# Moving two up-projection slices of the next expert ahead of the broadcast matmuls in an eight-expert feed-forward kernel

## The chip, the cores and the metric

The kernel runs on the 8 cores of one Trainium2 chip, two dies of four cores. All cores run the same program on different data and do not talk to each other. The metric is the device time of the slowest core in microseconds. TensorE is called PE in the profile, VectorE DVE, ScalarE ACT, GpSimd POOL and SyncE SP.

## The reference

```python
def reference(...):
    x = L0_attn_x                      # (4, 4096, 1024)
    x = x + _L0_attn_ref(_layernorm(x), Wd, bd, Wi, bi, gamma, beta)   # gated diagonal scan over time
    x = x + _L0_ffn_ref(_layernorm(x), router_w, w1, b1, w2, b2, gamma, beta)
...
# _L0_ffn_ref, 8 experts, every expert computed for every token, D = 1024, D_FF = 4096
    gates = ...                        # softmax over the top 2 of 8 router logits, 0 elsewhere
    h = gelu(einsum('nd,edf->enf', x, w1) + b1)
    out = einsum('enf,efd->end', h, w2) + b2
    res = x[None] + out
    mu, var = mean(res), mean(square(res - mu))
    expert_out = (res - mu) * rsqrt(var + 1e-6) * gamma + beta
    y = einsum('end,ne->nd', expert_out, gates)
```

The change touches only the expert part. For each expert it needs two big products, a normalization of each token over its 1024 features, and a sum over experts weighted by the gates.

## The kernel before

Each core owns 2048 tokens and first runs the scan stage (about the first 800 us). Then come the experts, in two groups of GT = 1024 tokens (`for g in range(n_groups)`), and in each group 8 experts (`for ee in range(n_experts)`). Features lie on the partitions and tokens on the free axis, so the means over the features are made by matmuls with a column of ones.

The kernel is written against a small recorder (`Rec`). `r.emit(engine, ...)` appends an instruction to one engine's list ("t" PE, "v" DVE, "s" ACT), `r.dma("y"/"q", ...)` a transfer issued by SP or POOL, and `r.wait(engine, token)` a semaphore wait. Each engine runs its own list strictly in the order in which it was written down. So the place of a Python statement sets its place in each engine's queue and nothing else.

One pass of the expert loop, expert `ee`:

- **B(ee)**, L885: out = w2 * h. Per half `th` of 512 tokens it takes 16 blocks `kb` of w2, each of 2 x 8 matmuls: 256 matmuls of 128x512 per half, 512 per expert. The 8 PSUM banks hold the 8 feature tiles, bank `m2` for tile `m2`, in the order 0 to 7. The first matmul into each bank waits on `bank_free[m2]`. DVE moves the sums out as `res_b` (L894, 8 per half).
- **A(ee+1), slice 0**: `emit_A_ms(ee + 1, 0)`. A slice of the up-projection is 128 matmuls (L836) in 16 runs of 8, which take banks 4 and 5 in turn; after each run ACT writes a 128x512 piece of `h_b` by Gelu (L842) and frees the bank. An expert has four slices `ms`.
- The gates of the expert are transposed into a row (L911) and copied to `g_r` (L916). Sums over res_b (L928) and over its squares (L936 on ACT, L945 on PE) go to banks 0 to 3, row 0.
- **A(ee+1), slice 1**, behind these on PE.
- **Row chain**, `rows_combine` (helper, lines 226 to 258) and three more: mean and variance of 1024 tokens in one row on DVE (L237 to L240), square root on ACT (L245), reciprocal (L249) and nm_r (L250) on DVE, then u1, u2 and the gate row in bf16 (L960, L962, L964). Their token is `urows_v`.
- **Broadcast**, L971: 6 matmuls with a row of ones spread u1, u2 and g over 128 partitions, into banks 0 to 3, 6 and 7. The first waits on `urows_v`.
- **y pass**, L982, L984, L987, L992 on DVE: 16 times these four operations of 128x512, which read the broadcast banks and add the expert's weighted output to `yacc`. Its last token is `y_v`:

```python
            y_v = r.token("v")
            res_read_tok = y_v
            prev_y_v = y_v
            for b_ in (0, 1, 2, 3, 6, 7):
                bank_free[b_] = y_v
```

- **A(ee+1), slices 2 and 3**, the last in the pass. Then B(ee+1) begins; it needs `h_done_s` and, in its first matmuls, the banks 0 to 7.

The last expert of a group has no A(ee+1), so there are 7 x 2 = 14 passes with one and 2 without. In these two the y pass is followed by the transposes of the output (L1029).

Weights: w1 comes in slices of 1024 columns into two buffers (`prefetch_w1`, issued at the head of the slice before it: POOL in group 0, which converts from f32, L623, and SP stores the bf16 copy to DRAM, L629; SP in group 1, L635). w2 comes in 16 blocks per half into three buffers (`prefetch_w2`: POOL L650 for the first half in group 0, otherwise SP L662).

Of the kernel before, what the change touches and what calls it, by code (L numbers as in the profile page):

```python
# [111 lines left out]
def build_nc(n_tiles=N_SST, n_groups=NG, n_experts=E, taps=None):  # L112
# [25 lines left out]
    r = Rec(nc, stack)  # L138
# [4 lines left out]
    def tap(name, ap, tok):  # L143
        if name not in tap_set:
            return
        dt_ = ap.dtype
        dr = nc.dram_tensor("tap_" + name, list(ap.shape), dt_,
                            kind="ExternalOutput").ap()
        r.wait("y", tok)
        ttok = r.dma("y", "ost", lambda e, dr=dr, ap=ap: e.dma_start(dr, ap))  # L150
        for engk in ("t", "v", "s", "q", "y"):
            r.wait(engk, ttok)
# [31 lines left out]
    def bank(i):  # L184
        return pall[:, i * 512:(i + 1) * 512]
# [430 lines left out]
    def prefetch_w1(ee, ms, g):  # L616
        par = w1_round[0] % 2
        r.wait("q", w1_free[par])
        r.wait("y", w1_free[par])
        r.wait("q", w1_slot_store[par])  # L620
        r.wait("y", w1_slot_store[par])
        if g == 0:
            tok = r.dma("q", f"w1{par}", lambda e, ee=ee, ms=ms, par=par: e.dma_start(  # L623
                w1bufs[par][:].rearrange("p (kk f) -> p kk f", kk=FC),
                w1[ee, :, ms * 1024:(ms + 1) * 1024].rearrange(
                    "(kk p) f -> p kk f", p=128)))
            r.wait("y", tok)
            stok = r.dma("y", f"w1s{par}", lambda e, ee=ee, ms=ms, par=par:
                         e.dma_start(w1s_dram[ee, ms], w1bufs[par][:]))  # L629
            w1s_tok[(ee, ms)] = stok  # L630
            w1_slot_store[par] = stok
        else:
            r.wait("y", w1s_tok[(ee, ms)])
            tok = r.dma("y", f"w1h{par}", lambda e, ee=ee, ms=ms, par=par:
                        e.dma_start(w1bufs[par][:], w1s_dram[ee, ms]))  # L635
        w1_round[0] += 1
        return tok, par
# [39 lines left out]
    for g in range(n_groups):  # L677
# [135 lines left out]
        def emit_A_ms(ee, ms):  # L813
            nonlocal w1tok, w1par
            cur_tok, cur_par = w1tok, w1par
            if ms < 3:
                w1tok, w1par = prefetch_w1(ee, ms + 1, g)
            elif ee < n_experts - 1:
                w1tok, w1par = prefetch_w1(ee + 1, 0, g)
            elif g == 0 and NG > 1:  # L820
                w1tok, w1par = prefetch_w1(0, 0, 1)
            else:
                w1tok, w1par = None, None
            r.wait("t", cur_tok)
            r.wait("t", xn2_v)
            for m in range(FC):
                for nt in range(2):
                    b_ = 4 + (m * 2 + nt) % 2
                    r.wait("t", bank_free[b_])
                    for kk in range(FC):  # L830
                        lhs = w1bufs[cur_par][:, kk * 1024 + m * 128:
                                              kk * 1024 + (m + 1) * 128]
                        rhs = xn2_b[:, kk * GT + nt * 512:
                                    kk * GT + nt * 512 + 512]
                        r.emit("t", lambda e, l=lhs, rr=rhs, b_=b_, kk=kk:
                               e.matmul(bank(b_), l, rr, start=(kk == 0),  # L836
                                        stop=(kk == FC - 1)))
                    mm_t = r.token("t")
                    fo = ms * 8 + m
                    r.wait("s", mm_t)  # L840
                    r.emit("s", lambda e, fo=fo, nt=nt, b_=b_, ee=ee:
                           e.activation(  # L842
                               h_b[:, fo * 1024 + nt * 512:
                                   fo * 1024 + nt * 512 + 512],
                               bank(b_), AF.Gelu,
                               bias=b1_c[:, ee * 32 + fo:ee * 32 + fo + 1]))
                    bank_free[b_] = r.token("s")
            w1_free[cur_par] = r.token("s")
# [4 lines left out]
        h_done_s = r.token("s")  # L853
        a_mm_tok = r.token("t")

        for ee in range(n_experts):
# [44 lines left out]
            last_in_group = ee == n_experts - 1  # L901
# [62 lines left out]
            r.emit("v", lambda e: e.tensor_copy(g_rb[0:1, :], g_r[0:1, :]))  # L964
            urows_v = r.token("v")

            r.wait("t", urows_v)
            for nt in range(2):
                for b0, row in ((0, u1_rb), (2, u2_rb), (6, g_rb)):
# [28 lines left out]
            prev_y_v = y_v  # L998
            for b_ in (0, 1, 2, 3, 6, 7):
                bank_free[b_] = y_v  # L1000

            if not last_in_group:
                for ms in range(2, 4):
                    emit_A_ms(ee + 1, ms)
                h_done_s = r.token("s")
                a_mm_tok = r.token("t")
            tap(f"res_b{g}_{ee}", res_b[:], res_v)
            tap(f"g_r{g}_{ee}", g_r[0:1, :], urows_v)
            tap(f"rs_r{g}_{ee}", rs_r[0:1, :], urows_v)
# [93 lines left out]
```

How the kernel before makes its waits and increments, by code:

```python
            def body(e):  # L93
                done = 0
                for kind, fn, name, val in self.ops[eng_key]:
                    if kind == "wait":
                        e.wait_ge(self.sems[name], val)
                    else:
                        if ser and kind == "op" and done > 0:
                            e.wait_ge(own, done)
                        fn(e).then_inc(self.sems[name], val)
                        if kind == "op":
                            done += val
```

## Time and profile before

| | |
|---|---|
| median of 2 runs | 5792.02 us (5790.36 to 5793.69) |
| profiled execution, own time | 5787.88 us |
| its span, first to last instruction, slowest core (core 4) | 5786.0 us |
| spans of the 8 cores | 5766.1 to 5786.0 us |
| PE busy | 4373.2 us, 76% of the span |
| DVE, ACT busy | 1663.6 and 1125.9 us |

The page gives one execution on the slowest core. A group row names line, engine, operation and tiles; then busy time and mean of one, and the idle time of the engine just before them with what ended it. Matmuls are pipelined: the listed length of one (about 380 ns) is longer than its step from one to the next. The timeline merges neighbours, so a row may stand for many instructions.

### The profile page before, as it was taken

To read this page: it belongs to the slowest core of one execution; us is meant where nothing else is said; L and a number is where in the kernel's file an instruction comes from. 1 tells how busy PE (TensorE), PEld (TensorE's weight loads), DVE (VectorE), ACT (ScalarE), POOL (GpSimd) and SP (SyncE) were. 2 spreads that over 40 slices of the span, in tenths; PEclk is the share of its full clock that TensorE was granted. 3 is DMA by queue.
4 is the path that set the end of the run, shared out by engine and by line. 5 is a ranking of instruction groups with operands and counts; after the bars stand their busy time and mean duration, and the time that the engine had idled before them with its cause. 6 is when DMAs were issued, how large, how long until landed. Compare 5 with 4: busy or idle time off the path is not lost.

```text
span 5786.0 us, 49875 instructions; the slowest of 8 cores (5766.1 to 5786.0 us)
## 1 busy us (share of the span) xinstructions
PE 4373.2 (76%) x18678; PEld 1883.7 (33%) x19040; DVE 1663.6 (29%) x2165; ACT 1125.9 (19%) x1429; POOL 161.7 (3%) x199
## 2 busy tenths in 40 slices
PE   1874516888888888888787527989888888889893
PEld 0321202333333333333333213434333333334341
DVE  0456532022221313131313351040413140413225
ACT  0332312020212121212111003031212122121210
POOL 0001000000000000000000000000000000000000
PEclk9997758989898989999999758999999999989896
DMA  6100042847475656574746211313132222223231
GB/s 75 44 30 15 29 102 59 185 113 171 120 162 129 157 131 153 127 164 115 166 123 138 77 73 51 124 62 127 65 110 80 95 95 87 94 89 102 80 95 40
DMA packets 229019, 586.59 MB, mean 101 GB/s; under 512 B 75056, under 2 KB 75184, under 8 KB 220592
## 3 DMA queue, kind: packets, MB, share of 16 engines
q1 hardware_dynamic: 157568, 444.95, 22.1%
q0 software_dynamic: 71216, 138.44, 15.6%
q8 instruction: 156, 2.56, 0.2%
q14 instruction: 79, 0.65, 0.0%
HBM read 570.77 MB, written 150.99 MB: 125 GB/s over the span
## 4 chain that ended last, share of the span: by engine, by line
PE 67%; DVE 14%; DMA 9%; ACT 4%; issue 3%; SPq 2%; DVEq 0%; ACTq 0%; POOLq 0%
PE pall L836 31%; PE pall L885 26%; DMA w2buf<-w 7%; PE pall L424 3%; DVE res_b L894 3%; DVE rs_r L249 3%; ACT sq_b L936 2%; PE pall L945 2%; DMA yacc<-xmid_scr 1%; PE pall L928 1%; SPq L201 1%; PE pall L334 1%; DVE xn_b L387 1%; PE pall L971 1%; DVE nm_r L250 1%
## 5 line engine op out<-in xcount | busy, mean ns | idle before, releaser
L885 PE MATMUL pall<-h_b,w2buf 128*128 128x512 bf16 x8020 | 1858.9, 389 | 230.9 <-DMA w2buf<-w 136.5
L836 PE MATMUL pall<-xn_b,w1buf 128*128 128x512 bf16 x8026 | 1849.1, 392 | 144.7 <-ACT h_b L842 67.0
L842 ACT ACTIVATE h_b<-pall,b_c 128x512 bf16<-128x512 f32 x1024 | 703.3, 688 | 3026.0 <-PE pall L836 3025.6
L885 PEld LDWEIGHTS pall<-h_b,w2buf 128*128 128x128 bf16 x8192 | 807.1, 100 | 1282.7 <-issue 392.7
L836 PEld LDWEIGHTS pall<-xn_b,w1buf 128*128 128x128 bf16 x8192 | 818.1, 100 | 1185.6 <-issue 283.3
L894 DVE SCALAR_TENSOR_TENSOR res_b<-pall,b_c,xn_b 128x512 bf16<-128x512 f32 x256 | 192.2, 751 | 2296.0 <-PE pall L885 2271.6
L424 PE MATMUL pall<-xn_b,WdWi_b 128*128 128x512 bf16 x1000 | 236.1, 395 | 128.8 <-ACT dec L434 70.4
L249 DVE RECIPROCAL rs_r<-rs_r 1x1024 f32<-1x1024 f32 (+1 forms) x30 | 157.8, 5261 | 503.6 <-ACT rs_r L245 503.6
L971 PE MATMUL pall<-u_rb,ones_row_b 1*128 1x512 bf16 x64 | 33.0, 616 | 244.8 <-DVE g_rb L964 244.8
L987 DVE SCALAR_TENSOR_TENSOR yacc<-sq_b,fgam_c,yacc 128x512 f32<-128x512 f32 x256 | 192.3, 751 | 29.6 <-DVE sq_b L984 3.7
L992 DVE SCALAR_TENSOR_TENSOR yacc<-pall,fbet_c,yacc 128x512 f32<-128x512 f32 x256 | 192.2, 751 | 26.7
L982 DVE TENSOR_TENSOR sq_b<-res_b,pall 128x512 f32<-128x512 bf16 x256 | 176.1, 688 | 73.6 <-PE pall L971 48.6
L936 ACT ACTIVATE sq_b<-res_b 128x2048 bf16<-128x2048 bf16 x64 | 122.1, 1908 | 381.1 <-DVE res_b L894 276.8
L424 PEld LDWEIGHTS pall<-xn_b,WdWi_b 128*128 128x128 bf16 x1024 | 101.6, 101 | 264.2 <-issue 157.1
L984 DVE TENSOR_TENSOR sq_b<-sq_b,pall 128x512 f32<-128x512 f32 x256 | 176.0, 688 | 26.7
L945 PE MATMUL pall<-sq_b,ones_col_b 128*1 128x512 bf16 x256 | 92.7, 501 | 103.8 <-ACT sq_b L936 103.8
L916 DVE COPY g_r<-pall 1x1024 f32<-1x1024 f32 x16 | 19.4, 1212 | 407.5 <-PE pall L911 407.5
L314 PE MATMUL pall<-ident,xt 128*128 128x128 f32 x256 | 40.7, 307 | 118.7 <-DMA xt<-ssm_x 110.1
L237 DVE COPY nm_r<-pall 1x1024 f32<-1x1024 f32 (+1 forms) x30 | 29.9, 998 | 344.1 <-PE pall L945 232.7
L650 POOL DMA_DIRECT2D w2buf<-w x128 | 90.1, 705 | 1178.1 <-PE pall L885 1122.4
L1029 PE MATMUL pall<-ident,yacc 128*128 128x128 f32 x128 | 28.1, 406 | 125.2 <-DVE yacc L992 106.2
L460 DVE TENSOR_TENSOR_SCAN states<-dec,carry,inj 128x512 f32<-128x512 f32 x64 | 82.1, 1284 | 81.8 <-ACT inj L439 78.3
(104 smaller groups left out, 1235.8 us busy)
## 6 DMA issues: line engine op xcount, KB each, us to landing
w2buf<-w2s_scr SPq DMA_DIRECT2D x384, 512.0 KB, 3.7
w1buf<-w POOLq DMA_DIRECT2D x32, 2048.0 KB, 16.0
w1s_scr<-w1buf SPq DMA_DIRECT2D x32, 2048.0 KB, 6.3
w2buf<-w POOLq DMA_DIRECT2D x128, 512.0 KB, 8.3
w2s_scr<-w2buf SPq DMA_DIRECT2D x128, 512.0 KB, 6.6
w1buf<-w1s_scr SPq DMA_DIRECT2D x32, 2048.0 KB, 7.9
xt<-ssm_x SPq DMA_DIRECT2D x8, 2048.0 KB, 9.3
xmid_scr<-x_f SPq DMA_DIRECT2D x4, 2048.0 KB, 7.2
```

The source lines that it names most:

```text
L249: r.emit("v", lambda e: e.reciprocal(rs_r[0:1, 0:n], rs_r[0:1, 0:n]))
L424: r.emit("t", lambda e, l=lhs, rr=rhs, b_=b_, kk=kk: e.matmul(bank(b_), l, rr, start=(kk == 0), stop=(kk == FC - 1)))
L836: e.matmul(bank(b_), l, rr, start=(kk == 0), stop=(kk == FC - 1)))
L842: e.activation(h_b[:, fo * 1024 + nt * 512: fo * 1024 + nt * 512 + 512], bank(b_), AF.Gelu, bias=b1_c[:, ee * 32 + fo:ee * 32 + fo + 1]))
L885: e.matmul(bank(m2), l, rr, start=(kk2 == 0), stop=(kk2 == 31)))
L894: e.scalar_tensor_tensor(res_b[:, sl], bank(m2), b2_c[:, ee * 8 + m2:ee * 8 + m2 + 1], xn2_b[:, sl], ALU.add, ALU.add))
L936: r.emit("s", lambda e, half=half: e.activation(sq_b[:], res_b[:, half * 2 * GT:(half + 1) * 2 * GT], AF.Square))
L945: r.emit("t", lambda e, rr=rhs, fcg=fcg, nt=nt: e.matmul(pall[0:1, 1024 + nt * 512: 1024 + nt * 512 + 512], ones_col_b[:], rr, start=(fcg ...
L982: r.emit("v", lambda e, sl=sl, nt=nt: e.tensor_tensor(tscr[:, 0:512], res_b[:, sl], bank(0 + nt), ALU.mult))
L984: r.emit("v", lambda e, nt=nt: e.tensor_tensor(tscr[:, 0:512], tscr[:, 0:512], bank(2 + nt), ALU.add))
L987: e.scalar_tensor_tensor(yacc[:, sl], tscr[:, 0:512], fgam_c[:, ee * 8 + fc:ee * 8 + fc + 1], yacc[:, sl], ALU.mult, ALU.add))
L992: e.scalar_tensor_tensor(yacc[:, sl], bank(6 + nt), fbet_c[:, ee * 8 + fc:ee * 8 + fc + 1], yacc[:, sl], ALU.mult, ALU.add))
```

## The change

The block that emits slices 2 and 3 of the next expert's up-projection is moved from behind the y pass to a place ahead of the wait on `urows_v`. Nothing is added or removed. Lines 967 to 1000 of the file shift by six in the new version (the broadcast is L977 there, the y pass L988 to L998).

```diff
@@ -964,6 +964,12 @@
             r.emit("v", lambda e: e.tensor_copy(g_rb[0:1, :], g_r[0:1, :]))
             urows_v = r.token("v")
 
+            if not last_in_group:
+                for ms in range(2, 4):
+                    emit_A_ms(ee + 1, ms)
+                h_done_s = r.token("s")
+                a_mm_tok = r.token("t")
+
             r.wait("t", urows_v)
             for nt in range(2):
                 for b0, row in ((0, u1_rb), (2, u2_rb), (6, g_rb)):
@@ -998,12 +1004,6 @@
             prev_y_v = y_v
             for b_ in (0, 1, 2, 3, 6, 7):
                 bank_free[b_] = y_v
-
-            if not last_in_group:
-                for ms in range(2, 4):
-                    emit_A_ms(ee + 1, ms)
-                h_done_s = r.token("s")
-                a_mm_tok = r.token("t")
             tap(f"res_b{g}_{ee}", res_b[:], res_v)
```

The queue of PE over one pass before, from B of one expert to B of the next (u_rb stands for u1_rb and u2_rb, xn_b for xn2_b, a row for as many equal matmuls as its x says):

```order
L885 MATMUL pall<-h_b,w2buf 128x512 x512
L836 MATMUL pall<-xn_b,w1buf 128x512 x128
L911 MATMUL pall<-ident,gates_tok 1x128 x8
L928 MATMUL pall<-res_b,ones_col_b 1x512 x16
L945 MATMUL pall<-sq_b,ones_col_b 1x512 x16
L836 MATMUL pall<-xn_b,w1buf 128x512 x128
L971 MATMUL pall<-u_rb,ones_row_b 128x512 x2
L971 MATMUL pall<-g_rb,ones_row_b 128x512
L971 MATMUL pall<-u_rb,ones_row_b 128x512 x2
L971 MATMUL pall<-g_rb,ones_row_b 128x512
L836 MATMUL pall<-xn_b,w1buf 128x512 x256
L885 MATMUL pall<-h_b,w2buf 128x512 x512
```

The same stretch of PE's queue in the changed kernel:

```order
L885 MATMUL pall<-h_b,w2buf 128x512 x512
L836 MATMUL pall<-xn_b,w1buf 128x512 x128
L911 MATMUL pall<-ident,gates_tok 1x128 x8
L928 MATMUL pall<-res_b,ones_col_b 1x512 x16
L945 MATMUL pall<-sq_b,ones_col_b 1x512 x16
L836 MATMUL pall<-xn_b,w1buf 128x512 x384
L977 MATMUL pall<-u_rb,ones_row_b 128x512 x2
L977 MATMUL pall<-g_rb,ones_row_b 128x512
L977 MATMUL pall<-u_rb,ones_row_b 128x512 x2
L977 MATMUL pall<-g_rb,ones_row_b 128x512
L885 MATMUL pall<-h_b,w2buf 128x512 x512
```

The 256 matmuls of slices 2 and 3 have moved from behind the six broadcasts to ahead of them, and the broadcasts now stand directly before B.

The second place is the seam before B, with the waits that each instruction carries (`__v` is DVE's semaphore, `__s` ACT's, w22 that of a w2 buffer), as a piece of the difference:

```order
 L836 MATMUL pall<-xn_b,w1buf 128x512 [waits __s]
 L836 MATMUL pall<-xn_b,w1buf 128x512 x7
+L977 MATMUL pall<-u_rb,ones_row_b 128x512 [waits __v]
+L977 MATMUL pall<-u_rb,ones_row_b 128x512
+L977 MATMUL pall<-g_rb,ones_row_b 128x512
+L977 MATMUL pall<-u_rb,ones_row_b 128x512 x2
+L977 MATMUL pall<-g_rb,ones_row_b 128x512
 L885 MATMUL pall<-h_b,w2buf 128x512 [waits w22,__s,__v]
 L885 MATMUL pall<-h_b,w2buf 128x512 x15
```

B's first matmul carries a wait on DVE in both kernels; what moved is that the broadcasts, on which DVE's y pass waits, now come immediately ahead of it. The queues of ACT, POOL and SP are the same in both, and DVE's differs in line numbers only.

## Rows read from the trace of the kernel before

**Rows 1.** The page: busy time by engine, and the chain that ended last, by line.

```profile
PE 4373.2 (76%) x18678; PEld 1883.7 (33%) x19040; DVE 1663.6 (29%) x2165; ACT 1125.9 (19%) x1429; POOL 161.7 (3%) x199
PE pall L836 31%; PE pall L885 26%; DMA w2buf<-w 7%; PE pall L424 3%; DVE res_b L894 3%; DVE rs_r L249 3%; ACT sq_b L936 2%; PE pall L945 2%; DMA yacc<-xmid_scr 1%; PE pall L928 1%; SPq L201 1%; PE pall L334 1%; DVE xn_b L387 1%; PE pall L971 1%; DVE nm_r L250 1%
```

**Rows 2.** Who waited for whom, whole span: us in total, times, longest.

```profile
PE pall L971 <- DVE g_rb L964: 244.8, 16, 18.1
...
PE pall L885 <- DMA w2buf<-w: 136.5, 83, 3.9
...
PE pall L1029 <- DVE yacc L992: 106.2, 2, 53.3
...
PE pall L836 <- ACT h_b L842: 67.0, 16, 31.0
```

**Rows 3.** Timeline, a pass of group 1: slice 1, row chain, broadcast, slice 2.

```profile
4077.83 9.66 PE L836 MATMUL pall<-xn_b,w1buf 128*128 128x512 bf16 x43
...
4088.30 1.28 ACT L245 ACT_TABLE_LOAD   x1
4089.59 1.15 ACT L245 ACTIVATE rs_r<-rs_r,eps_c 1x1024 f32<-1x1024 f32 x1
...
4101.51 0.68 DVE L964 CAST g_rb<-g_r 1x1024 bf16<-1x1024 f32 x1
...
4102.34 1.01 PE L971 MATMUL pall<-u_rb,ones_row_b 1*128 1x512 bf16 x2 [14.84 <-DVE g_rb L964]
...
4104.98 5.52 PE L836 MATMUL pall<-xn_b,w1buf 128*128 128x512 bf16 x16
...
4105.23 0.69 DVE L982 TENSOR_TENSOR sq_b<-res_b,pall 128x512 f32<-128x512 bf16 x1 [3.04 <-PE pall L971]
...
4108.65 1.28 ACT L842 ACT_TABLE_LOAD   x1 [17.92 <-PE pall L836]
...
4109.95 1.34 ACT L842 ACTIVATE h_b<-pall,b_c 128x512 bf16<-128x512 f32 x2
...
4111.00 51.74 PE L836 MATMUL pall<-xn_b,w1buf 128*128 128x512 bf16 x235 [0.50 <-ACT h_b L842]
```

**Rows 4.** Timeline, the end of the same pass and the start of B.

```profile
4157.08 0.75 DVE L992 SCALAR_TENSOR_TENSOR yacc<-pall,fbet_c,yacc 128x512 f32<-128x512 f32 x1
...
4162.84 0.69 ACT L842 ACTIVATE h_b<-pall,b_c 128x512 bf16<-128x512 f32 x1 [1.04 <-PE pall L836]
...
4163.78 2.32 PE L885 MATMUL pall<-h_b,w2buf 128*128 128x512 bf16 x10 [1.04 <-ACT h_b L842]
```

**Rows 5.** Timeline, last pass of group 0: last broadcast, end of the y pass, next PE work.

```profile
3304.29 0.63 PE L971 MATMUL pall<-g_rb,ones_row_b 1*128 1x512 bf16 x1
...
3357.30 0.75 DVE L992 SCALAR_TENSOR_TENSOR yacc<-pall,fbet_c,yacc 128x512 f32<-128x512 f32 x1
...
3358.20 1.09 PE L1029 MATMUL pall<-ident,yacc 128*128 128x128 f32 x4 [53.28 <-DVE yacc L992]
```

**Rows 6.** Stretches, PE: from:to, us, busy (count), granted clock share, DMA share, GB/s.

```profile
3132.00:3141.00 9.00, 8.70 (x32) 0.81 1.01 203
...
926.70:932.00 5.30, 5.29 (x15) 0.59 0.00 0
932.00:940.00 8.00, 7.95 (x38) 1.00 0.00 0
...
4102.30:4108.60 6.30, 6.26 (x15) 0.50 0.00 0
```

**Rows 7.** Timeline, first expert of group 0: a w1 load on POOL, PE through the slices.

```profile
982.18 0.88 POOL L623 DMA_DIRECT2D w1buf<-w  x1 [26.75 <-ACT h_b L842]
...
926.71 109.34 PE L836 MATMUL pall<-xn_b,w1buf 128*128 128x512 bf16 x486 [30.97 <-ACT h_b L842]
```

**Rows 8.** Timeline, PE in the first half of a B of group 0.

```profile
3131.94 8.75 PE L885 MATMUL pall<-h_b,w2buf 128*128 128x512 bf16 x32 [2.22 <-DMA w2buf<-w]
```

## The prediction

> **What bounds the kernel now.** I read the page first. PE is busy for 76% of the span, and the chain that ended last lies on the two expert products, L836 31% and L885 26% [rows 1]. PE is the bound in the expert part, so the question is always what PE waits for. The waits view answers it: 16 waits of L971 for the DVE row chain (L964) cost 244.8 us, 15.3 us each; B waits 136.5 us for w2, all of it in first halves of group 0; and twice PE waits 53 us for the y pass, where an output transpose follows it directly [rows 2]. The timeline of one pass shows the first of these. Slice 1 ends at 4077.83 + 9.66 = 4087.49. ACT loads a table and takes the root until 4090.74, DVE has the rows at 4102.19, and PE starts the broadcasts at 4102.34 after 14.84 us of idling [rows 3]. During this wait the 256 matmuls of slices 2 and 3, which need nothing of the rows, stand behind the broadcast in PE's queue. They run from 4104.98 to 4162.74, and beside them DVE runs the y pass from 4105.23 to 4157.08 + 0.75 = 4157.83. B starts at 4163.78, waiting only 1.04 us for the last Gelu [rows 3, 4]. So slices 2 and 3 are the cover of the y pass, and the cover is 5 us longer than what it hides.
>
> **The change part by part.** It puts slices 2 and 3 into the 14.84 us gap, and takes them away from the y pass. Both ends are worked out from the pass in rows 3 and 4; zero is the same end of slice 1, 4087.49.
>
> Slices 2 and 3. At full clock a matmul steps every 51.74 / 240 = 0.2156 us (235 records stand for the 240 behind the first 16) [rows 3]. The first two runs of 8 take 16 x 0.2156 = 3.45 us, to 4090.94, since banks 4 and 5 are free by then. The third needs the Gelu of the first. ACT's order is unchanged: root until 4090.74, table back to Gelu 1.28 us, Gelu 1.34 / 2 = 0.67 us, then 0.35 us until PE goes on (before: Gelu done at 4110.65, PE at 4111.00) [rows 3]. That gives 4093.1, a PE stop of 2.1 us. The other 240 matmuls take 51.7 us: 4144.8. Such a stop can lower the clock: after a DMA gap of 2.22 us in group 0, 32 matmuls took 8.75 us, not 7.0 [rows 8], at a granted clock of 0.81 [rows 6]. I bound this by 0 and 1.7 us and take 0.4, since that stretch has gaps one after another and here a full slice runs before and two behind.
>
> On the table load the trace shows 1.28 us each time and the next ACTIVATE right behind it (4088.30 + 1.28, root at 4089.59); the load itself began 0.81 us after slice 1's last matmul, which is one Gelu [rows 3]. The Trainium skill, page "ScalarE: Activation LUTs", section "What ACT_TABLE_LOAD costs", counts a drain of about 1.38 us on top, 2.66 us per switch. By that the exposed switch would add an estimated 14 x 1.38 = 19 us to the result; by the row it adds nothing beyond the 1.28.
>
> The weights for slice 3. Its load is issued when slice 1's last Gelu frees the buffer, as before, but is needed 14.8 + 2.9 us earlier, that is after 28 us. In the first expert of group 0, slices run back to back with just that lead (POOL issues one at 982.18, 26.75 us of idle behind the last), and PE ran 486 records in 109.34 us without a wait for w1 [rows 7]. Cost nothing; if it were late by the 5 us by which the cover fails, 7 passes would pay 35 us.
>
> Broadcasts. At the low clock the six matmuls took 2.64 us (4102.34 to 4104.98), and DVE started 0.25 us later, at 4105.23 [rows 3]. They now come behind warm work: 6 x 0.216 + 0.25 = 1.6 us, and DVE starts the y pass at 4144.8 + 1.6 = 4146.4 (between 1.6 and 2.9 us; I take 1.6).
>
> The y pass. 64 operations took 4157.83 - 4105.23 = 52.6 us [rows 3, 4]. Behind them on PE, where nothing covers them, they took the same: last broadcast issued at 3304.29, its 0.63 us, then 53.28 us of idle PE [rows 5]. It ends at 4146.4 + 52.6 = 4199.0.
>
> B. All of banks 0 to 3, 6 and 7 get `y_v`, the token of the whole pass, and B's first matmul takes bank 0. PE starts 3358.20 - 3358.05 = 0.15 us behind the last y operation [rows 5]: B at 4199.2 against 4163.8 before. That is 35.4 us later. PE then comes out of 53 us of idling. In group 0 it came out of 30.97 us, and the granted clock was 0.59 for 5.3 us, then 1.00 [rows 6, 7]; behind the present 14.84 us it was 0.50 for 6.3 us [rows 6]. The first costs 5.3 x 0.41 = 2.2 us, the second 3.1 us; the present one is already inside 4163.8, the new one comes on top. I take 2.2, between 1 and 4.
>
> What else waits for B is DVE (res_b) and the w2 buffers; nothing is queued behind them that ends elsewhere, so they shift with it. In group 0 the three w2 buffers are filled before B today too: no DMA wait stands at B's start [rows 4]. I cost this at 0, between -4 and +1 us for those seven passes.
>
> Sum: 35.4 + 2.2 + 0.4 = 38.0 us per pass, 14 passes, 532 us. On the profiled execution's own 5787.9 us that gives 6320; the median of the runs shown is 4 us above it, so **6324 us**.
>
> Matmuls in the trace start in their queue's order; the 256 independent ones stood still behind the broadcast for 14.84 us [rows 3]. The Trainium skill, page "TensorE: Matmul & The Clock Gate", section "Step-by-step: what each phase is for", says the same in general: matmuls stay in program order and only weight loads are pulled ahead. It speaks against the change: B, once it waits for bank 0, lets nothing pass. Were it otherwise, the first rival's time would hold.
>
> **The rivals.**
>
> *The y pass hides under B, faster.* The place is B's first wait. If it were not bound by the y pass, B would start right behind the broadcasts at 4146.4, 17.4 us earlier than today: 5792 - 14 x 17.4 = 5548 us. It decides at that number: the change gains where what blocks bank 0 is shorter than 17.4 us behind the broadcasts, and loses beyond. For it speaks only that DVE is busy for 29% of the span [rows 1]. Against it: 52.6 us is three times 17.4, and the order shows B's first matmul with a wait on DVE. Chance 0.02.
>
> *The move is worth little either way*, because some of the pass is released early: it must bring the 38 us to under 8.3 (2% of 5792 over 14). No row supports it. 0.02. That the move isn't made can be left out, the order shows it.
>
> *The wait is refunded in group 0.* The w2 waits of B are 136.5 us over 8 experts [rows 2]. If the pause let the transfers catch up, 7 / 8 of it could go: 6324 - 119 = 6205 us. Against it: only three blocks of 16 fit ahead, and the waits recur through the half [rows 8]. 0.04.
>
> *The clock stays low longer after 53 us than after 31.* A matmul at the low clock takes 6.26 / 15 = 0.42 us [rows 6]. If the first 32 of B all do, each pass loses 32 x 0.20 = 6.4 us in place of 2.2: 6324 + 14 x 4.2 = 6383 us. The low level after both idle stretches lasted 5 to 6 us alike [rows 6], so 0.05.
>
> **How the numbers follow.** My forecast has the remaining 0.87. Its own spread: each pass 35.2 to 41.7 us, from the clock after the stop (+1.3), after the long wait (-1.2, +1.8), the broadcasts (+1.3) and the w2 and w1 transfers (-2, some +1), not all at one end: 6285 to 6375. The refund and most of the long cold start lie outside, with under 0.1 together. About 2%, 116 us, is what a measurement of this kernel can tell from no change. Slower by more holds in all but the first two rivals: 0.96; within 2% 0.02; faster 0.02.
>
> **What would show each step right or wrong.** In the changed kernel's waits, the wait of the broadcast on DVE stays in 2 passes only (36 us in all), and B has 14 new waits on DVE's L998 of some 53 us, 745 us together. In the timeline slices 2 and 3 are one row from slice 1 on, with one stop of 2.1 us behind 16 matmuls, and a pass of group 1 is 38 us longer. DVE stands still for 41 us more between L964 and L988. ACT loads the Gelu table right behind the root. The prediction is wrong if B starts while DVE is still at L998, if the stop at slice 2 is over 4 us, or if B's first half in group 0 shows clearly fewer w2 waits than 136.5 us.

## The result and the profile after

The changed kernel is slower: 1.094 times the kernel before, 95% interval 1.0921 to 1.0959. On 5792 us that is 6336 us (6325 to 6347 by the interval); the prediction was 6324 us. In 7 of its 11 executions, as in part of those of the kernel before, the cores of one die ran at a lower granted clock and took longer (the median of all 11 is 6563 us, outside the stated range of 6285 to 6375); such executions are left out here and in every comparison below, and the four others took 6333 to 6346 us.

| | before | after |
|---|---|---|
| span of the profiled execution, slowest core | 5786.0 us | 6354.2 us |
| core 4 in the same two executions | 5786.0 us | 6315.0 us |
| PE busy | 4373.2 us | 4401.3 us |
| DVE busy | 1663.6 us | 1662.6 us |

The columns compare core 4 before with core 2 after. PE does the same work, 18678 instructions in both, and on core 4 after the change it is busy for 4373.1 us, as before; the added time is idle time. The page of the kernel after, its busy row, the row of group B, and the chain:

```profile
PE 4401.3 (69%) x18678; PEld 1894.9 (30%) x19040; DVE 1662.6 (26%) x2165; ACT 1124.2 (18%) x1429; POOL 161.4 (3%) x199
...
PE 61%; DVE 21%; DMA 8%; issue 4%; ACT 3%; SPq 1%; DVEq 1%; ACTq 0%; POOL 0%; POOLq 0%
...
L885 PE MATMUL pall<-h_b,w2buf 128*128 128x512 bf16 x8020 | 1919.9, 398 | 959.4 <-DVE yacc L998 743.0
```

DVE has the same busy time but 21% of the chain, and the idle time before B is now named after the last operation of the y pass. The waits of the kernel after (us in total, times, longest):

```profile
PE pall L885 <- DVE yacc L998: 743.0, 14, 53.3
DVE sq_b L988 <- PE pall L977: 628.7, 16, 48.4
...
PE pall L885 <- DMA w2buf<-w: 134.0, 67, 5.9
...
PE pall L836 <- ACT h_b L842: 88.5, 16, 30.7
...
PE pall L977 <- DVE g_rb L964: 36.3, 2, 18.1
```

These answer to [rows 2]. The wait for the row chain has fallen from 16 times to the 2 passes that have no slices to run (36.3 us); in its place stand 14 waits of 53 us for the y pass. The w2 waits of group 0 are what they were (134.0 against 136.5 us). In the timeline of a pass of group 1 on core 2 (start, length, what; the idle time before it in brackets), slices 1 to 3, broadcasts and B on PE:

```profile
4367.22 32.35 PE L836 MATMUL pall<-xn_b,w1buf 128*128 128x512 bf16 x141 [0.33 <-issue]
4401.51 51.96 PE L836 MATMUL pall<-xn_b,w1buf 128*128 128x512 bf16 x235 [1.94 <-ACT h_b L842]
4453.40 0.60 PE L977 MATMUL pall<-u_rb,ones_row_b 1*128 1x512 bf16 x2
...
4507.75 4.42 PE L885 MATMUL pall<-h_b,w2buf 128*128 128x512 bf16 x10 [52.89 <-DVE yacc L998]
4512.40 53.47 PE L885 MATMUL pall<-h_b,w2buf 128*128 128x512 bf16 x241 [0.22 <-issue]
4566.94 0.38 PE L885 MATMUL pall<-h_b,w2buf 128*128 128x512 bf16 x1 [1.07 <-DVE res_b L894]
```

and ACT and DVE at the stop behind the second run of slice 2, with the rows (L964) ready and the y pass (L988) not started:

```profile
4396.92 1.28 ACT L245 ACT_TABLE_LOAD   x1
4398.22 1.15 ACT L245 ACTIVATE rs_r<-rs_r,eps_c 1x1024 f32<-1x1024 f32 x1
4399.38 1.28 ACT L842 ACT_TABLE_LOAD   x1
4400.68 1.27 ACT L842 ACTIVATE h_b<-pall,b_c 128x512 bf16<-128x512 f32 x2
...
4410.14 0.68 DVE L964 CAST g_rb<-g_r 1x1024 bf16<-1x1024 f32 x1
...
4455.04 0.69 DVE L988 TENSOR_TENSOR sq_b<-res_b,pall 128x512 f32<-128x512 bf16 x1 [44.22 <-PE pall L977]
```

The rows lie ready for 42.6 us (4410.82 to 4453.40), since the broadcasts stand behind the slices, and then PE stands idle for 53.

How much a pass costs is read best from one DVE instruction that comes once per pass, the copy of the gate row (L916). On core 4 of the kernel before, three in a row of group 1:

```profile
3769.61 1.21 DVE L916 COPY g_r<-pall 1x1024 f32<-1x1024 f32 x1 [29.16 <-PE pall L911]
...
4043.02 1.21 DVE L916 COPY g_r<-pall 1x1024 f32<-1x1024 f32 x1 [28.10 <-PE pall L911]
...
4319.04 1.21 DVE L916 COPY g_r<-pall 1x1024 f32<-1x1024 f32 x1 [29.28 <-PE pall L911]
```

and two on core 4 of the kernel after:

```profile
4338.33 1.21 DVE L916 COPY g_r<-pall 1x1024 f32<-1x1024 f32 x1 [29.20 <-PE pall L911]
...
4652.36 1.21 DVE L916 COPY g_r<-pall 1x1024 f32<-1x1024 f32 x1 [29.20 <-PE pall L911]
```

Before, three of the six regular passes of group 1 take 273.4 to 273.5 us and three 276.0 to 276.5, 274.8 on average; after, each takes 314.0 us. That is 39.2 us more. From the first such copy to the last, over all 14 passes and the seam between the groups, core 4 goes from 4450.8 us (1216.88 to 5667.68) to 4990.6 us (1205.05 to 6195.65): 539.8 us. The seam has 3.1 of them; the 14 passes have 536.7, or 38.3 each: 37.6 in group 0 and 39.0 in group 1. Core 4's whole span in the table grew by only 529 us because its first copy came 11.8 us earlier after the change. Over the eight cores the stretch from first to last copy grew by 523 to 568 us.

### The profile page after: what moved, and what is told of

Read it like the earlier page. It is cut to its first block, busy times and chain, and to the rows that moved or that the text cites. A ratio compares the mean times of both kernels' runs of the same rounds, so it can differ in the third digit from the quotient of the medians.

```text
span 6354.2 us, 49875 instructions; the slowest of 8 cores (6295.9 to 6354.2 us)
## 1 busy us (share of the span) xinstructions
PE 4401.3 (69%) x18678; PEld 1894.9 (30%) x19040; DVE 1662.6 (26%) x2165; ACT 1124.2 (18%) x1429; POOL 161.4 (3%) x199
## 4 chain that ended last, share of the span: by engine, by line
PE 61%; DVE 21%; DMA 8%; issue 4%; ACT 3%; SPq 1%; DVEq 1%; ACTq 0%; POOL 0%; POOLq 0%
PE pall L836 27%; PE pall L885 25%; DMA w2buf<-w 6%; DVE yacc L993 3%; DVE yacc L998 3%; PE pall L424 3%; DVE sq_b L988 3%; DVE sq_b L990 3%; DVE res_b L894 3%; ACT sq_b L936 1%; PE pall L945 1%; DVE rs_r L249 1%; PE pall L928 1%; DMA yacc<-xmid_scr 1%; SPq L201 1%
## 5 line engine op out<-in xcount | busy, mean ns | idle before, releaser
L885 PE MATMUL pall<-h_b,w2buf 128*128 128x512 bf16 x8020 | 1919.9, 398 | 959.4 <-DVE yacc L998 743.0
L836 PE MATMUL pall<-xn_b,w1buf 128*128 128x512 bf16 x8026 | 1830.1, 389 | 166.8 <-ACT h_b L842 88.5
L885 PEld LDWEIGHTS pall<-h_b,w2buf 128*128 128x128 bf16 x8192 | 823.7, 101 | 2055.5 <-issue 1243.8
L988 DVE TENSOR_TENSOR sq_b<-res_b,pall 128x512 f32<-128x512 bf16 x256 | 175.9, 687 | 653.7 <-PE pall L977 628.7
L998 DVE SCALAR_TENSOR_TENSOR yacc<-pall,fbet_c,yacc 128x512 f32<-128x512 f32 x256 | 192.0, 750 | 26.7
L916 DVE COPY g_r<-pall 1x1024 f32<-1x1024 f32 x16 | 19.4, 1211 | 411.0 <-PE pall L911 411.0
L334 PE MATMUL pall<-x_f,ones_col_f 128*1 128x512 f32 x128 | 66.5, 680 | 31.6 <-DVE xn_b L387 28.3
```

The costliest lines, as they stand in the source:

```text
L836: e.matmul(bank(b_), l, rr, start=(kk == 0), stop=(kk == FC - 1)))
L885: e.matmul(bank(m2), l, rr, start=(kk2 == 0), stop=(kk2 == 31)))
L988: r.emit("v", lambda e, sl=sl, nt=nt: e.tensor_tensor(tscr[:, 0:512], res_b[:, sl], bank(0 + nt), ALU.mult))
L998: e.scalar_tensor_tensor(yacc[:, sl], bank(6 + nt), fbet_c[:, ee * 8 + fc:ee * 8 + fc + 1], yacc[:, sl], ALU.mult, ALU.add))
```

## The experiments

The first five take apart where the wait comes from; the others move the root or free the banks. A pass is the step between two gate copies of group 1, read on core 0 in each profile, and so are the timelines; the waits views are of the slowest core. Ratios are to runs of the kernel before on the same chip; those took 5796 to 5805 us.

**Half of the y pass left out, in both kernels.** If the y pass stands uncovered before B in the changed kernel and covered in the one before, half of it must be worth time in one and next to nothing in the other.

```diff
             r.wait("v", ebc_t)
-            for fc in range(FC):
+            for fc in range(FC // 2):
```

On the changed kernel:

> The changed kernel with the y pass cut to features 0 to 3 of 8 (32 of its 64 operations; the output therefore misses half of what the experts add, the loads and matmuls are all there). Theory, the y pass stands uncovered before B: each of the 14 passes loses 32 operations, 26.3 us, and so do the 2 passes at the ends of the groups: 6336 - 16 x 26.3 = 5915 us; PE's wait of B on DVE falls from 53 to about 27 us in 14 passes. Rival, the time is lost by the stop at slice 2, the weight loads or the clock: only the 2 end passes gain, 6336 - 53 = 6283 us.

On the kernel before:

> The kernel before with the same half of the y pass left out (output misses the same half). Theory: its y pass lies under slices 2 and 3, so only the 2 end passes gain 26.3 us each: 5792 - 53 = 5739 us. If the y pass cost time in the other passes too, up to 5792 - 421 = 5371 us.

Measured on the changed kernel: ratio 1.0187 (1.0165 to 1.0209), the two executions 5908 and 5913 us (5915 expected). A pass takes 286.7 us, 27.3 less. The waits of its profile:

```profile
PE pall L885 <- DVE yacc L998: 374.1, 14, 26.9
```

For the kernel before there is a single execution, 5742.3 us, 3 us from the expected time; its passes still take 273.4 to 276.5 us, the times of the full y pass. So the y pass is under slices 2 and 3 there and is paid in full in the changed kernel. The rival (6283 us) is out.

**One slice ahead instead of two.**

```diff
             urows_v = r.token("v")
+            if not last_in_group:
+                emit_A_ms(ee + 1, 2)
...
             if not last_in_group:
-                for ms in range(2, 4):
+                for ms in range(3, 4):
                     emit_A_ms(ee + 1, ms)
```

> Half of the change: slice 2 ahead of the broadcast, slice 3 behind the y pass. Theory: with slice 1's end at 4087.5, slice 2 ends at 4087.5 + 27.6 + 2.1 = 4117.2, DVE starts the y pass at 4118.8 and ends it at 4171.4, slice 3 is done at 4146; B starts at 4171.6 against 4163.8, some 25 us of idle PE before it and then 2 to 3 us of low clock: +10 us a pass, 5792 + 140 = 5932 us. Rival, each slice ahead of the broadcast costs by itself (stop at the root, earlier need of w1): half of the change, 5792 + 272 = 6064 us.

Measured: ratio 1.0273 (1.0254 to 1.0291), 5955 to 5967 us, a pass of 286.7 us, 11.9 more than before (10 expected). B waits 25 us for the y pass:

```profile
PE pall L885 <- DVE yacc L995: 355.0, 14, 25.5
```

One slice costs 0.3 of what two cost, not half. The cost is not proportional to the slices moved; it begins where the cover that is left (here slice 3, 27.6 us) is shorter than the y pass (52.6 us).

**Half a slice ahead.** The broadcasts are written into the middle of slice 2; its second half and slice 3 stay behind them.

```diff
-        def emit_A_ms(ee, ms):
+        def emit_A_ms(ee, ms, pause=None):
...
                     bank_free[b_] = r.token("s")
+                    if pause is not None and m * 2 + nt == 7:
+                        pause()
...
-            r.wait("t", urows_v)
-            for nt in range(2):
+            def bcast():
+                r.wait("t", urows_v)
+                for nt in range(2):
...
+            emit_A_ms(ee + 1, 2, pause=bcast)
```

> Only the first 8 of the 16 runs of slice 2 (64 matmuls) ahead of the broadcast, the other 8 and slice 3 behind it. Theory: they take 13.8 + 2.1 us and end at 4103.4, about when the rows are there (4102.2); the y pass starts at 4105.0 as before and ends at 4157.6; PE is done at 4146 and waits about 11 us for it; B at 4157.8 against 4163.8, with 2 us of low clock behind the wait: -4 us a pass, 5792 - 56 = 5736 us. Rival, matmuls ahead of the broadcast cost time by themselves: not under 5792 us.

Measured: ratio 0.9943 (0.9926 to 0.9961), 5765 to 5771 us, so 33 us faster and not 56: clear of 1, but less than 2%. A pass takes 273.1 us, 1.8 less. PE:

```profile
4342.66 10.52 PE L836 MATMUL pall<-xn_b,w1buf 128*128 128x512 bf16 x47 [1.94 <-ACT h_b L842]
4353.11 0.60 PE L974 MATMUL pall<-u_rb,ones_row_b 1*128 1x512 bf16 x2
...
4407.48 4.42 PE L887 MATMUL pall<-h_b,w2buf 128*128 128x512 bf16 x10 [11.36 <-DVE yacc L1001]
```

The broadcasts no longer wait, and B now waits 11.4 us for the y pass. From the start of slice 1 (4308.34) B comes 99.1 us later, against 4163.78 - 4058.79 = 105.0 us in the pass of [rows 3, 4]: 5.9 us earlier, as expected (6.0). What is missing is behind it: B's first half takes 59.4 us (4407.48 to 4466.91) in place of 56.5, so 2.9 us of low clock after the wait and not 2, and the pass compared with was one of the longer kind. Filling the gap is worth something, but only until the y pass is the later of the two; moving PE's work alone does not win the gap of 14.8 us as long as the y pass keeps the banks.

**Work in the wait.** This measures what the low clock behind the wait costs.

```diff
             ebc_t = r.token("t")
             prev_ebc_t = ebc_t
+            if not last_in_group:
+                r.wait("t", bank_free[4])
+                for i_ in range(240):
+                    r.emit("t", lambda e, i_=i_: e.matmul(
+                        bank(4), xn2_b[:, 0:128], xn2_b[:, 0:512],
+                        start=True, stop=True))
```

> The changed kernel with 240 matmuls of 128x512 added between the broadcasts and B, into bank 4, whose results nobody reads: 51.7 us of work in a wait of 53. Theory: B starts at the same time but at full clock, and the first half of B falls from 59.2 us to 56.5: 6336 - 14 x 2.7 = 6298 us. Rival, the low clock behind the wait costs nothing or the added work delays B: 6336 us or more.

Measured: ratio 1.0861 (1.0838 to 1.0884), 6295 and 6302 us (6298 expected); a pass takes 310.6 us in place of 314.0. B starts at full speed:

```profile
4427.93 51.97 PE L987 MATMUL pall<-xn_b 128*128 128x512 bf16 x235
4480.93 55.41 PE L885 MATMUL pall<-h_b,w2buf 128*128 128x512 bf16 x251 [1.03 <-DVE yacc L1005]
```

The same 251 records took 58.1 us in the kernel after (4.42, a gap of 0.22 and 53.47), 2.7 more. Filling the wait gives back 3.4 us of the 39.2 a pass; 2.7 of them are in B's first half, the other 0.7 is not located. The wait itself is nearly all the rest.

**The root ahead of slice 1**, on the kernel before and on the changed one.

```diff
+            rowsdone = rows_combine(pall[0:1, 0:1024], pall[0:1, 1024:2048],
+                                    EPS2, False, deps=[est_t, prev_ebc_t])
+            for b_ in range(4):
+                bank_free[b_] = rowsdone[0]
             if not last_in_group:
                 emit_A_ms(ee + 1, 1)
-            rowsdone = rows_combine(...)
-            for b_ in range(4):
-                bank_free[b_] = rowsdone[0]
```

On the kernel before:

> The kernel before with rows_combine written ahead of slice 1 (the root stands before slice 1's Gelus in ACT's queue), the rest as before. Theory, the 14.8 us wait for the rows comes from the root's place in ACT's queue, and the y pass keeps its cover: root at about 4063, rows at about 4075, in time for the broadcasts behind slice 1 at 4090.8 (slice 1 gets a stop of about 3.3 us), slices 2 and 3 end at 4147.3, y pass at 4145, B at 4148.2 against 4163.8: -15.6 us a pass, 5792 - 218 = 5574 us. Rival, the gap is given back as low clock or as w2 waits in group 0: 5680 to 5792 us.

On the changed kernel:

> The changed kernel with the same root ahead of slice 1. Theory: the rows are ready earlier still, but the y pass waits for the broadcasts behind slice 3 as before: the stop moves from slice 2 (2.1 us) to slice 1 (3.3 us), 6336 + 14 x 1.2 = 6353 us. Rival, the rows' lateness is what costs: down towards 5574 us.

On the kernel before: ratio 0.9704 (0.9683 to 0.9724), 5620 and 5634 us, between the 5574 expected and the rival's 5680; a pass of 262.8 us, 12.0 less and not 15.6. PE and ACT of one pass:

```profile
4205.99 4.70 PE L836 MATMUL pall<-xn_b,w1buf 128*128 128x512 bf16 x15 [0.33 <-issue]
4214.34 26.02 PE L836 MATMUL pall<-xn_b,w1buf 128*128 128x512 bf16 x110 [3.64 <-ACT h_b L842]
4240.29 0.60 PE L972 MATMUL pall<-u_rb,ones_row_b 1*128 1x512 bf16 x2
...
4298.15 55.41 PE L885 MATMUL pall<-h_b,w2buf 128*128 128x512 bf16 x251 [1.04 <-ACT h_b L842]
```

```profile
4209.75 1.28 ACT L245 ACT_TABLE_LOAD   x1 [6.10 <-DVE rs_r L240]
4211.05 1.15 ACT L245 ACTIVATE rs_r<-rs_r,eps_c 1x1024 f32<-1x1024 f32 x1
```

The wait of 14.8 us is gone and B waits only for its last Gelu, as before the change. But ACT stands idle for 6.1 us until DVE has the variance, and only then loads the table, while slice 1's Gelus queue behind it: PE's stop is 3.6 us, and the granted clock is 0.72 in the 15 matmuls before it and 0.65 in the 3.7 us behind it, where the kernel before has no stop. On the changed kernel the same edit gives a single execution, 6393.5 us against 6353 expected, and a pass of 317.4 us, 3.4 longer than without it (1.2 expected). The rows are ready 26 us earlier there (17.7 us after the start of slice 1 in place of 43.6), B still waits for the y pass 14 times, 743.3 us in all, and nothing is gained: the lateness of the rows is not what costs.

**The banks freed by a copy.** The order of the changed kernel, but the y pass no longer holds the banks.

```diff
+            r.wait("s", ebc_t)
+            r.wait("s", prev_bcs_v)
+            for i_, b_ in enumerate((0, 2, 6, 1, 3, 7)):
+                o_ = (i_ % 3) * GT + (i_ // 3) * 512
+                r.emit("s", lambda e, o_=o_, b_=b_: e.activation(
+                    bcs[:, o_:o_ + 512], bank(b_), AF.Copy))
+            bcs_s = r.token("s")
...
             for b_ in (0, 1, 2, 3, 6, 7):
-                bank_free[b_] = y_v
+                bank_free[b_] = bcs_s
+            prev_bcs_v = y_v
```

The y pass reads `bcs` (bf16) in place of the banks, and the rows u1 and u2 share the tiles of rs_rb and nm_rb to make room.

> The changed kernel, but ACT copies the six broadcast banks to SBUF as bf16 and the banks are freed by the copies, not by the y pass; the y pass reads the copies. Theory, B waits for the banks alone: six copies of 0.69 us behind the broadcasts, B at about 4146.3 + 4.4 = 4150.7 against 4163.8, the y pass under B: -13 us a pass, 5792 - 182 = 5610 us. Rival, B waits for DVE for another reason or the y pass beside B is slowed: 5792 us or more.

Measured: ratio 0.9714 (0.9693 to 0.9735), 5630 to 5649 us, a pass of 262.8 us.

```profile
4335.99 0.37 PE L979 MATMUL pall<-g_rb,ones_row_b 1*128 1x512 bf16 x1
4339.65 57.10 PE L887 MATMUL pall<-h_b,w2buf 128*128 128x512 bf16 x251 [3.29 <-ACT bcs L990]
...
4339.67 0.69 DVE L998 TENSOR_TENSOR sq_b<-res_b,bcs 128x512 f32<-128x512 bf16 x1 [47.36 <-ACT bcs L990]
```

B starts 3.3 us behind the last broadcast, and DVE starts the y pass beside it and ends it at 4392.42, still within B's first half. With the banks released early the changed order is 2.9% faster than the kernel before, the six copies (3.0 us) included. This is the rival of the prediction that came out faster, brought about by taking its obstacle away: what decided between a loss of 9.4% and a gain of 2.9% is the release of six banks. It gains 12.0 us a pass and not the 17.4 of that rival or the 13 expected here: B starts later by the copies, and its first half takes 1.7 us longer (57.10 against 55.41) at a granted clock of 0.68 in its first 5.4 us. The kernel before with the same copies was not run.

**A better version.** The root in the middle of slice 1, the rest as before; then, on top, banks 4 and 5 moved out first behind B.

```diff
+                    if pause is not None and m * 2 + nt == 5:
+                        pause()
...
+            def combine():
+                rowsdone.extend(rows_combine(...))
+                for b_ in range(4):
+                    bank_free[b_] = rowsdone[0]
...
+                emit_A_ms(ee + 1, 1, pause=combine)
```

> The kernel before with rows_combine written behind the first 6 of the 16 runs of slice 1. Theory: DVE has rs_r by then, so ACT's root no longer waits for it, PE is at full clock at the stop, and the stop is 2.1 us instead of the 3.6 us and some low clock of the version with the root ahead of all of slice 1; rows ready well before slice 1 ends. A pass of group 1 takes 260.5 us against 262.9 there and 274.8 before; 5797 - 14 x 14.3 = 5597 us, ratio 0.9655. Rival, the stop costs the same wherever the root stands: pass 262.9, ratio 0.970.

```diff
-                for m2 in range(FC):
+                for m2 in ((4, 5, 0, 1, 2, 3, 6, 7) if th == 1 else range(FC)):
                     sl = slice(m2 * GT + th * 512, m2 * GT + th * 512 + 512)
```

> The same, and behind the second half of B DVE moves out banks 4 and 5 first, which slice 0 of the next expert takes. PE's wait there, 4.5 us (the fifth bank moved out), falls to the first, about 1.1 us, less low clock behind it: -3.4 us a pass, 257.1 us; 5797 - 14 x 17.7 = 5549 us, ratio 0.957. Rival, PE then waits at the next use of a bank and nothing is gained: as without it.

The first: ratio 0.9611 (0.9592 to 0.9629), 5570 to 5578 us (5597 expected), a pass of 259.4 us, 15.4 less than before. The stop in slice 1 is 1.94 us, with a granted clock of 1.00 before and behind it. The second has a single execution to compare, 5506.4 us, beside 5796 to 5805 us of the kernel before, and a pass of 252.6 us, where 257.1 was expected. Slice 0 behind B with the first edit alone, and with both:

```profile
4407.59 30.53 PE L836 MATMUL pall<-xn_b,w1buf 128*128 128x512 bf16 x126 [4.49 <-DVE res_b L896]
```

```profile
4315.81 27.79 PE L836 MATMUL pall<-xn_b,w1buf 128*128 128x512 bf16 x126 [1.08 <-DVE res_b L896]
```

The wait falls by 3.4 us, and the slice behind it by 2.7: the granted clock in its first 5.4 us was 0.50 with the first edit alone and is 1.00 with both, so the short wait had also cost a stretch of low clock. Of the 6.8 us a pass these two are 6.1. How much of the total time the second edit is worth rests on this single execution.

## Why the prediction was right and where it was wrong

- **The bound and the cover: right.** Slices 2 and 3 hide the y pass before, and nothing hides it after; the half y pass in both kernels shows it from both sides.
- **The stop at slice 2: right.** 2.1 us predicted, 1.94 us measured. The 240 matmuls behind it took 51.96 us against 51.74 at a granted clock of 1.00, so the clock did not fall; of the 0.4 us allowed, at most 0.2 came, and the kernel before has 51.96 in another pass too (3837.55). The table loads carried no drain: root and Gelu each follow their load directly (4396.92 + 1.28, root at 4398.22; 4399.38 + 1.28, Gelu at 4400.68), and the 19 us by the Trainium skill's page "ScalarE: Activation LUTs", section "What ACT_TABLE_LOAD costs", did not come.
- **Weights for slice 3 and the w2 refund: right.** No wait for w1 appears, and the w2 waits stayed at 134 us. The refund rival is out. For the start of B in group 0 the prediction points at [rows 4], which is a pass of group 1; the trace shows the same there, the seven B of group 0 that follow slices start behind a wait of 1.0 to 1.1 us for the last Gelu and none for w2.
- **Broadcasts and y pass: right.** From the start of slice 1 B comes at 4507.75 - 4367.22 = 140.5 us, against 105.0 in [rows 3, 4]: 35.5 us later. Predicted were 35.4, and 0.4 for the clock behind the stop, which lies in this stretch.
- **Low clock behind the wait: a little small.** B's first half took 59.2 us (4507.75 to the next row at 4566.94) in place of 56.5, so 2.7 us and not 2.2; filling the wait with work gave back 3.4 us a pass. The prediction took the 5.3 us at a granted clock of 0.59 from group 0; here they are at 0.50 (from:to, length, busy, granted clock, DMA share, GB/s), and 5.3 x 0.50 = 2.7. The rival of a long low clock (4.2 us more) is out.

```profile
4507.70:4513.00 5.30, 5.03 (x12) 0.50 0.01 3
4513.00:4520.00 7.00, 7.00 (x34) 0.98 0.28 97
```

- **The pass compared with: a small term that was mis-sized.** The step "both ends are worked out from the pass in rows 3 and 4" took one pass for the typical one. It lies in a pass of 276.0 us between gate copies (4043.02 to 4319.04); half of the regular ones take 273.4 us. The changed passes of group 1 take 314.0 us, and 314.0 - 276.0 = 38.0 is the predicted loss. Against the mean of 274.8 it is 39.2 us, so this term was 1.2 us too small. In group 0 the loss was 37.6 us on core 4, and the 14 passes and the seam together are 539.8 us against 532 predicted. That is 8 of the 12 us by which 6324 falls short of 6336; the rest is not assigned and is smaller than the differences between cores. What makes the two kinds of pass is the clock. On core 4, with the same wait of 4.49 us before slice 0 in both:

```profile
4012.50 1.99 PE L836 MATMUL pall<-xn_b,w1buf 128*128 128x512 bf16 x6 [4.49 <-DVE res_b L894]
4014.70 27.26 PE L836 MATMUL pall<-xn_b,w1buf 128*128 128x512 bf16 x119 [0.22 <-issue]
...
4287.34 30.65 PE L836 MATMUL pall<-xn_b,w1buf 128*128 128x512 bf16 x126 [4.49 <-DVE res_b L894]
...
4012.50:4018.00 5.50, 5.28 (x17) 0.69 0.00 0
4287.30:4292.80 5.50, 5.46 (x13) 0.50 0.01 1
```

  The slice takes 29.5 us in the pass of 273.4 us and 30.7 in that of 276.0. The first 244 records behind the bank hand-over in B's second half differ by another 1.6 us (54.99 and 56.59). The rest of the pass differs by 0.2 us the other way, which makes the 2.6 us. In the changed passes of group 1 on that core slice 0 takes 30.6 us every time, as in the slower kind.
- **The base and the range: the step that failed.** The step "the median of the runs shown is 4 us above it" took the 5792 us of two executions as the base of the sum, and neither the sum nor the range has a term for executions in which a die runs at a lower granted clock. The runs showed a median over all executions of 5973 us for the kernel before (10 executions, 5790 to 6366 us), 181 us above that base, and of 6563 us for the changed one (11 executions, 6333 to 7019 us). So the base was the term that was far off; the loss added to it, 532 us, compares with 544 us on the like executions (6336 us, inside the range) and with 590 us between the two medians, which also hold how often and how far the clock fell in each set. Why it falls, and what it falls to, no run here shows. That 6336 is only 12 us from the forecast is partly luck: the loss was larger than 38.0 us a pass in group 1 (39.0 on core 4) and smaller in group 0 (37.6).
- **The rival on the other side** was rightly placed at B's first wait. When the banks are freed early, the change gains, though less than it said: 5548 us worked out, 5630 to 5649 us measured, the six copies included.

That the y pass blocks through the banks and not through DVE being busy is shown, by the copy experiment. Why the clock stays low longer in one kind of pass than in the other, and why only the slower kind appears after the change, is open: it was read from rows only and not tried.

## What to carry to other kernels

Work that stands behind a wait may be the cover of something else: before moving it into the gap, write down what runs beside it now and who needs that to be finished. Here a wait of 15 us was filled and a pass of 53 us laid bare, because it held the banks of the next stage. The same gap was won by moving the late producer (a root queued behind sixteen Gelus on ACT) instead of the idle engine's work. And a pass length is best taken as a mean over several passes, from an instruction that comes once in each.

## What the runs showed of the hardware

- In these runs ACT loads a table only when the instruction behind it has its input: with the root early, the load began after 6.1 us of idling on DVE's rs_r, not ahead of time, so the 1.28 us were added to the wait. The same holds for the Gelu table in [rows 3], whose load begins after 17.92 us of waiting for PE. In these kernels the semaphore wait stands ahead of the instruction that needs the table; a load placed ahead of the wait was not tried.
- What the low clock behind a wait costs did not grow with the length of the wait from 11 to 53 us. The first 251 records of B took 55.4 us behind 1 us of idling, and 2.9, 2.9, 2.2 and 2.7 us longer behind 11.4 (half a slice ahead), 25.2 (one slice), 26.6 (half y pass) and 52.9 us (the changed kernel), at a granted clock of 0.50 in the first 5.3 to 5.5 us of the first and the last. Behind shorter waits it varied: 1.7 us behind 3.3 us (copies, clock 0.68); behind the 4.5 us before slice 0 the matmuls that take 27.8 us behind 1.1 us took 29.5 us in some passes and 30.5 to 30.7 in others. Behind the stop of 1.94 us at full clock in slice 2 there was none.
- ACT copied a broadcast bank of 128x512 from PSUM to SBUF in 3.04 / 6 = 0.51 us, where 0.69 us had been expected.
- In the profiled execution of the changed kernel, core 2 took 312.9 us for its last stretch between gate copies (core 4: 287.2 us) at a granted clock of 0.78 against 0.86:

```profile
5921.59:6234.52 312.93, 238.46 (x924) 0.78 0.19 66
```

```profile
5908.46:6195.65 287.19, 212.70 (x924) 0.86 0.21 72
```

PE is busy 25.8 us longer there for the same 924 records, and the stretch is 25.7 us longer. Core 2 is the slowest core of that execution, whose time of 6355.8 us lies 20 us above 6336, and most of the 28 us by which PE's busy time in the first table grew are these. That is why passes and not spans were compared above.
